# Two layer normalisations of the last batch, moved from VectorE to ScalarE, between the exponentials of the first attention head

## What is computed

```python
h = _layernorm(x, axis=-1) * (1 + ca) + sa        # "c0", then the modulation
x = x + ga * _L1_attn_ref(h, gamma, beta, Wq, Wk, Wv, Wo)

def _L1_attn_ref(x, ...):
    xn = layer_norm(x, ln_gamma, ln_beta)         # "c1"
    q, k, v = heads(xn @ Wq), heads(xn @ Wk), heads(xn @ Wv)
    att = q @ k.T / 8 + alibi_bias
    return (softmax(att) @ v) @ Wo

def _layernorm(x, axis=-1, eps=1e-05):
    m = jnp.mean(x, axis=axis, keepdims=True)
    v = jnp.var(x, axis=axis, keepdims=True)
    return (x - m) / jnp.sqrt(v + eps)
```

## Time and profile before

| | us |
|---|---|
| median of 3 runs | 2284.05 |
| the three runs | 2276.24, 2284.05, 2284.23 |
| the profiled execution, its own time | 2262.21 |
| its span, first to last instruction | 2260.4 |
| TensorE busy in the span | 2172.6 (96%) |
| VectorE busy | 1811.6 (80%) |
| ScalarE busy | 1248.2 (55%) |
| GpSimd busy | 1385.5 (61%) |

### The profile page before, as it was taken

The page is one execution under the profiler, slowest core; times in us unless marked ns, Lnnn a source line. Parts: engine busy times, 40 slices in busy tenths (PEclk is TensorE's granted clock), DMA queues, the critical chain, the costliest instruction groups (busy, mean ns, idle before and its releaser), DMA issues. The chain is left out here.

```text
span 2260.4 us, 40689 instructions
## 1 busy us (share of the span) xinstructions
PE 2172.6 (96%) x10606; PEld 1381.5 (61%) x10607; DVE 1811.6 (80%) x4826; ACT 1248.2 (55%) x1690; POOL 1385.5 (61%) x751
## 2 busy tenths in 40 slices
PE   7989999999999999999999999999999999989995
PEld 4756756556556565665656656565565654449884
DVE  7788887888888888888888888888888887765555
ACT  2333344566666666666666666666666663434442
POOL 2212121777777787787877777787777776643331
PEclk9999999999999999999999999999999999999997
DMA  7050220000001000000100000010000000411114
GB/s 251 26 201 1 87 80 31 24 17 13 16 18 33 17 13 16 18 14 16 31 16 18 16 14 13 16 36 17 14 13 18 17 8 11 153 43 49 47 45 138
DMA packets 90664, 91.79 MB, mean 41 GB/s; under 512 B 22261, under 2 KB 75125, under 8 KB 90553
## 3 DMA queue, kind: packets, MB, share of 16 engines
q1 hardware_dynamic: 86232, 81.88, 11.7%
q0 software_dynamic: 4352, 8.99, 1.2%
HBM read 57.90 MB, written 36.86 MB: 42 GB/s over the span
## 5 line engine op out<-in xcount | busy, mean ns | idle before, releaser
L1661 ACT ACTIVATE big<-P 128x1024 f32<-128x1024 f32 x512 | 512.6, 1021 | 99.6 <-PE P L2044 82.0
L2058 PE MATMUL P<-big,V 128*64 128x512 f32 x2048 | 470.5, 600 | 1.0 <-ACT big L1667 1.0
L658 POOL TENSOR_TENSOR spair<-spair,big 128x1024 f32<-128x1024 f32 x192 | 457.4, 2382 | 16.0 <-DVE hp L818 1.3
L658 POOL TENSOR_TENSOR opair<-opair,big 128x1024 f32<-128x1024 f32 x192 | 457.6, 2384 | 15.0
L1048 DVE CUSTOM_DVE_ANT_0 big<-P,near 128x512 f32<-128x512 f32 x512 | 349.0, 682 | 110.2 <-PE P L2028 107.7
L2028 PE MATMUL P<-kq 96*128 96x512 f32 x1008 | 414.2, 432 | 2.7 <-DVE kq L1036 1.4
L2043 PE MATMUL P<-kq 97*128 97x512 f32 x1024 | 409.5, 400 | 2.4 <-DVE xs L824 2.1
L1051 DVE TENSOR_REDUCE mhalf<-P 128x1 f32<-128x512 f32 x512 | 349.3, 682 | 76.7 <-PE P L2028 65.8
L2044 PE MATMUL P<-kq 128*128 128x512 f32 x1024 | 407.0, 397 | 0.0
L2028 PEld LDWEIGHTS P<-kq 96*128 96x128 f32 x1008 | 180.8, 189 | 204.1 <-issue 103.6
L2058 PEld LDWEIGHTS P<-big,V 128*64 128x64 f32 x2048 | 135.6, 137 | 266.3 <-issue 263.7
(11 more groups left out here) (333 smaller groups left out, 3636.2 us busy)
## 6 DMA issues: line engine op xcount, KB each, us to landing
slots<-later SPq DMA_DIRECT2D x4, 4224.0 KB, 16.1
kq<-auxrows SPq DMA_DIRECT2D x64, 128.0 KB, 2.2
wqk<-wparts SPq DMA_DIRECT2D x124, 64.0 KB, 1.8
big<-in_wex SPq DMA_DIRECT2D x8, 768.0 KB, 12.1
xt<-slots SPq DMA_DIRECT2D x76, 66.0 KB, 1.8
near<-in_aux SPq DMA_DIRECT2D x64, 64.0 KB, 1.8
big<-yrows SPq DMA_DIRECT2D x8, 512.0 KB, 7.2
xs<-in_x SPq DMA_DIRECT2D x4, 512.0 KB, 4.1
```

Of the source, the lines that this page charges most:

```text
L658: pool.tensor_tensor(psum8[s][:, :], psum8[s][:, :], pfull[:, j % RING, :], ALU.add).then_inc(S["p_added"], 1)
L1661: act.activation(pfull[:, j, :], banks(2 * (j % 2)), ACT.Exp, scale=DH1 ** -0.5).then_inc(S["exp_done"], 1)
L2058: mm = pe.matmul(P[64 * i:64 * i + 64, 4, :], V1[:, j, s, :], half(pfull[:, j, :], i), start=(j == 0), stop=(j == T - 1))
```

## The change

The last step of both normalisations of the last batch, 2 x 8 instructions of VectorE, becomes 2 x 8 activations of ScalarE: Identity(scale * x + bias) with scale = rstd and bias = -mean * rstd, both a column with one value for each partition. VectorE computes the bias column with one small instruction for each half (`c_shift`), in the place where `c_first` and `c_third` stood, into a part of `rlog` that is free then. ScalarE's groups (`c_norm`) stand between exponential 3 and the first value copy, and between exponentials 6 and 7. All readers keep their place and their waits on `ln_norm`. The semaphore `c_nmr` is one that is reused; it stands at 4 from the four routings of block 0.

```diff
@@ E, the table of reused semaphores
-             "c_kept": S["ydT_copied"], "t_gate": S["gates"], ...
+             "c_nmr": S["rb_lo"], "c_kept": S["ydT_copied"], "t_gate": S["gates"], ...
@@ block.vector
+            def c_shift(tag):
+
+                for i in range(NHALF):
+                    ts = slice(i * TPH, (i + 1) * TPH)
+                    dve.wait_ge(S["ln_rstd"], NHALF * LN_TAGS[tag] + i + 1)
+                    dve.scalar_tensor_tensor(rlog[:, ts, 0], mvs[1][:, ts, 0], -1.0, rstds[1][:, ts], ALU.mult, ALU.mult).then_inc(E["c_nmr"], 1)
+
             def c_second(b, halves=range(NHALF)):
...
             bias(0, 0, 3)
-            c_first(B - 1)
+            c_shift(f"c0{B - 1}")
             max_half(1, 1, 0, 0)
...
             bias(0, 0, 6)
-            c_third(B - 1)
+            c_shift(f"c1{B - 1}")
             max_half(1, 1, 1, 1)
@@ block.scalar
+            def c_norm(tag, nth, src, dst):
+
+                for t in range(T):
+                    if t % TPH == 0:
+                        act.wait_ge(E["c_nmr"], B + NHALF * nth + t // TPH + 1)
+                        act.wait_ge(S["ln_rstd"], NHALF * LN_TAGS[tag] + t // TPH + 1)
+                    act.activation(dst[:, t, :], src[:, t, :], ACT.Identity, bias=rlog[:, t, 0:1], scale=rstds[1][:, t:t + 1]).then_inc(S["ln_norm"], 1)
+
             def c_copies(b):
...
             exps(0, 3)
+            c_norm(f"c0{B - 1}", 0, tok(xs[:, B - 1, :]), xcs[B - 1])
             values(0, 0)
             q_again(1, 1)
             exps(0, 4)
...
             exps(0, 6)
+            c_norm(f"c1{B - 1}", 1, hcs[B - 1], xcs[B - 1])
             exps(0, 7)
```

More of the change, by code:

```diff
@@ L202, in network @@
         E = {**{f"t_out{i}": S[n] for i, n in enumerate(("wh_in0", "wh_in1", "wv_in", "hT_in")[:YBUF])}, **{f"m_y_in{b}": S[n] for b, n in enumerate(("aux_in0", "aux_in1", "tab_in0", "tab_in1"))}, "w_hi": S["vec_copied"], "w_lo": S["h_free"], "t_lo": S["xd_done"], "w_copy": S["next_mod"], "t_turned": S["turned"], "t_T": S["hT_act"], "t_w1": S["w1_mm"], "t_w3": S["w3_mm"], "t_silu": S["silu_done"],
-             "c_kept": S["ydT_copied"], "t_gate": S["gates"], "t_idx": S["dests"], "t_gu": S["gu_done"], "t_gu_turned": S["yd_turned"], "t_guT": S["hT_dve"],
+             "c_nmr": S["rb_lo"], "c_kept": S["ydT_copied"], "t_gate": S["gates"], "t_idx": S["dests"], "t_gu": S["gu_done"], "t_gu_turned": S["yd_turned"], "t_guT": S["hT_dve"],
              "t_down": S["downd_mm"], "t_y": S["ydT_copied"], "m_x_in": S["mod_in"],
```

## The result

The change makes the kernel slightly slower. Twelve runs of it have a median of 2281.76 us (2278.28 to 2285.99), twelve of the kernel before, now with nine more than were shown, 2276.52 us (2273.06 to 2284.23). The ratio is 1.0023, with a 95% interval of 1.0012 to 1.0034, so +2.7 to +7.7 us. The forecast was 2288.4 us, 6.6 us above what was measured.

What follows compares the result with a forecast made beforehand. TensorE, busy for 96% of the span, was taken as the bound, so delays to its stream arrive in full. A stall of 2.6 us plus 1.7 us of clock gave +4.3 us, 2288.4 us, range 2277 to 2296 us.

Steps and rivals of the forecast that it cites:

- The stall at the second value projection: TensorE waits there for ScalarE's first value copy, moved behind the first group: +2.6 us, bounds +1.1 to +3.3.
- The group on ScalarE: Eight Identity activations of 128x128 on ScalarE take 3.2 us, 0.48 us for one; bounds 1.7 to 3.8 us.
- The clock: Behind TensorE's stall a stretch at 0.50 clock loses 1.7 us, more likely than not; bounds 0 and 1.7 us.
- The sum: Stall of 2.6 us plus clock loss of 1.7 us gives +4.3 us.
- The second group: Between exponentials 6 and 7 on ScalarE it costs nothing; without TensorE's own delay as cover, 1.5 us.
- VectorE's relief: VectorE is relieved by 3.5 to 4.3 us, worth nothing on TensorE's path, bound 0.44 us.
- How the numbers follow: Closing step: a measurement tells 0.5%, 11.4 us, from no change; faster 0.03, within 0.92, slower 0.05.
- (1): Rival: TensorE's stall at the second value projection without the clock's fall, +2.6 us, 2286.7 us; chance 0.25.
- (2): Rival: scale and bias columns are cheap, a ScalarE group takes 1.7 us, +1.1 us, 2285.2 us; chance 0.08.
- (3): Rival: VectorE's relief shrinks TensorE's idle time up to 416.77 us, at most 1.8 us gained, 2282.3 us; chance 0.05.
- (4): Rival: TensorE waits once in each of the loop's 63 heads, 0.2 us each, 2299.3 us; chance 0.04.
- (5): Rival: Identity among ScalarE's exponentials loads a table, 1.28 us each time, 2289.7 us; chance 0.03.

Runs made afterwards that it cites:

- e3: The change plus eight matmuls on zeros ahead of the second value projection; passage 39.12 us, ratio to the kernel before 1.0000.
- e2: The change with the first group back on VectorE, only the second group on ScalarE; passage 36.63 us, ratio to the kernel before 1.0012.
- e11: Repeat of e2, only the second group on ScalarE; passage 35.24 us, ratio to the kernel before 1.0000.
- e5: The change with ScalarE's first group behind the first value copy and the duplicate of q behind exponential 4; passage 36.63 us, ratio to before 0.9995.
- e1: The change with the second group back on VectorE, only the first group on ScalarE; passage 39.25 us, ratio to the kernel before 1.0026.
- e8: The change itself measured again, against the kernel before; passage 40.69 us, ratio 1.0026.
- e12: e2 with VectorE's low parts of q and k and bias 3 ahead of the second half's statistics; passage 35.06 us, ratio to before 0.9994.
- e7: e5 with VectorE's low parts of q and k and bias 3 ahead of the second half's statistics; passage 35.25 us, ratio to before 0.9987.
- e6: The kernel before with VectorE's low parts of q and k and bias 3 ahead of the second half's statistics; passage 36.71 us, ratio 1.0001.
- e9: The kernel before measured against itself, with nothing changed; passage 36.63 us, ratio 0.9996.
- e10: Repeat of e3, the change with the stall filled by matmuls on zeros; passage 39.13 us, ratio to the kernel before 1.0002.
- e4: The change with four of the first group's eight tiles back on VectorE; passage 37.56 us, ratio to the kernel before 1.0003.

## Why the prediction was right or wrong

**Right: the mechanism and its size.** The stall at the second value projection: +2.6 us forecast, 2.41 us measured (T1), with the wait for the value copy shown in the row. The group on ScalarE, built from an exponential, two columns and an overlap: 3.2 us forecast, 3.18 us measured, 0.48 us and 0.483 us for one. The clock: 1.7 us forecast, 1.64 us in T2, of which e3 gives back 1.52. The sum: +4.3 us forecast, +4.05 us in the passage. The second group: nothing in the passage, shown by e2 and e11. VectorE's relief: nothing in the passage, shown by e5. VectorE got 0.63 us of new work where 0.8 us were set.

**Luck in the step on the clock.** The prediction argued that the clock would fall since the new stall is longer than the 2.1 us after which it had fallen. It did fall behind the stall of 2.25 us in all three traces that have it (after, e1, e8). But the argument is weaker than it looks: the same wait of 2.10 us at the head of the passage was followed by a fall in eleven of fourteen traces, and by none in e1, e11 and e12.

**Wrong: what the numbers were made to say.** The step "How the numbers follow" called 4 us, 0.19%, a difference inside what the measurement can tell, 0.5%, and put 0.92 on no change. With twelve runs a side the interval is 0.11% wide on either side, and a ratio of 1 lies outside it. The forecast time said slower, while the chances spoke as if it were nothing; faster had 0.03 and slower 0.05. The bound of 0.5% has no row behind it; the step only adds that three runs lay 8 us apart. This is the step that failed: the size was right, and it was called too small to be seen.

**Wrong in the sum against the times: the base.** The forecast added to the median of three runs, 2284.05 us; with twelve it is 2276.52 us. The step took the 21.8 us between the profiled execution and the median as a constant of the kernel. Of these, 7.5 us were the spread of three runs, and 14.3 us remain to the median of twelve, close to the difference between chips (16 to 17 us). With the base of twelve runs the same +4.3 us gives 2280.8 us, 0.9 us below the 2281.76 us measured. The stated range of 2277 to 2296 us held the result by its width, not by its middle.

**Missing: more of the lower clock, far away.** Between the loop's start and the router of block 1 the changed kernel takes 1503.04 us where the one before takes 1501.31 us. The windows from 1880 to 1925 us, of before, of after and of e7, in this order:

```profile
1880.00:1925.00 45.00, 41.79 (x158) 18.59 (x154) 35.25 (x124) 15.52 (x23) 28.95 (x24) 0.96 0.06 17
```

```profile
1880.00:1925.00 45.00, 40.35 (x153) 18.04 (x153) 32.56 (x108) 14.46 (x21) 28.56 (x20) 0.92 0.04 13
```

```profile
1880.00:1925.00 45.00, 40.96 (x163) 19.07 (x162) 36.33 (x137) 17.71 (x25) 30.18 (x24) 1.00 0.06 20
```

The granted clock is 0.96, 0.92 and 1.00: a stretch at the lower level in before (1889 to 1893 us), one of twice the time in after (1892 to 1900 us), none in e7. The time from the loop's start to the router follows it in all fourteen traces: 1499.72 us with 1.00 (e7), 1500.96 to 1501.60 us with 0.96 (before, e3, e6, e9, e10, e12), 1503.04 to 1503.45 us with 0.92 (after, e1, e2, e4, e5, e8, e11). So this is the 1.73 us. The four kernels that were profiled twice (before, the change, e2, e3) show the same value both times; what decides it is not shown. With it the profiled difference is 4.05 + 1.73 = 5.8 us, and the medians say 5.2 us. But e2, e4, e5 and e11 have 0.92 there as well, and timed ratios of 1.0012, 1.0003, 0.9995 and 1.0000, so this share is not in every timed run, and how much of it is in the median is not settled.

**The rivals.** (1), the stall without the clock, is what e3 makes by hand. (2), cheap columns, falls by 0.483 us. (3), relief that decides, falls by e5, and comes true in e7, where TensorE is early enough to wait for VectorE. (4), a loss in each head: from the loop's start to the router it is 1.73 us in all, 0.03 us a head, and it goes with the clock near the end. (5), a table load: none stands there.

## What to carry to other kernels

Work that is moved to an engine with idle time must be put into that idle time, not ahead of an instruction that another engine awaits: the same 3.2 us cost 4 us ahead of a copy with 0.4 us of slack, and nothing one place behind it, with the duplicate of q moved out of the way. An engine that is relieved returns time only where the bound engine waits for it; if there is no such wait, first take away what keeps the bound engine from coming early, then relieve. And when a forecast names a term of 4 us with a row for each part, ask how many runs resolve it before calling it no change.

## What the runs showed of the hardware

- An Identity with scale and bias as columns on 128x128 from SBUF lasts 0.483 us, and eight take 3.18 us, 0.385 us from start to start. That is 0.17 us more than the exponential of this size without columns (0.310 us), and neighbours overlap by 0.10 us.
- The clock's fall behind a stall of 2.25 us costs 1.5 us of dense TensorE work, on top of the 2.4 us of the stall itself, and eight matmuls on zeros prevent it (e3 and e10). A wait of 2.10 us was followed by a fall in eleven traces of fourteen.
- Between 1880 and 1925 us the time at the lower clock differs between kernels whose streams lie a few us apart: none, one stretch that costs about 1.7 us, or twice that. The cause is not shown.
- One late stretch takes 86.5 to 89.3 us on the chip of e1 to e4 and 102.8 to 107.1 us on the two others, the kernel before included; in the long ones engines wait for something that the profile does not find on the core, up to 9.4 us at a time.
